# Graph-network kernel: rows of a block spread over partitions, and a rearranged first stage and turn

## The reference

```
x = relu(layernorm(x));  z = layernorm(x) * ln1_g + ln1_b
q, k, v = z @ Wq + bq, z @ Wk + bk, z @ Wv + bv          # 8 heads of 64
scores[e, h] = q[dst[e], h] . k[src[e], h] / 8 + edge_attr[e, h]
alpha = softmax of scores over the edges that share dst
out = segment_sum(alpha * v[src], dst) @ Wo + bo
```

## Time and profile before

| | us |
|---|---|
| median of 3 runs | 410.22 |
| profiled execution | 413.15 |
| its span, first to last instruction | 411.7 |
| PE busy in it | 379.6 (92%) |
| DVE busy | 317.4 (77%) |
| ACT busy | 166.7 (40%) |
| mean granted TensorE clock | 0.987 |

### The profile page before, as it was taken

The page is one execution under the profiler, slowest core; times in us unless marked ns, Lnnn a source line. Parts: engine busy times, 40 slices in busy tenths (PEclk is TensorE's granted clock), DMA queues, the critical chain, the costliest instruction groups (busy, mean ns, idle before and its releaser), DMA issues.

```text
span 411.7 us, 5093 instructions
## 1 busy us (share of the span) xinstructions
PE 379.6 (92%) x1785; PEld 286.7 (70%) x1785; DVE 317.4 (77%) x668; ACT 166.7 (40%) x274; POOL 2.2 (1%) x13
## 2 busy tenths in 40 slices
PE   2779998889899999999999999999799999999994
PEld 1555564456567788889767878887668878787873
DVE  5797998789893968899795988399875678488346
ACT  1624444534522623334655934243362631135410
POOL 2000000000000000000000000000000000000000
PEclk9999999999998999999999999999989999999989
DMA  7503786777882600006900060500230023000002
GB/s 240 228 1 59 103 104 102 111 99 97 116 107 57 228 0 2 1 2 211 369 35 1 0 205 0 204 2 0 64 142 0 2 75 130 0 2 0 2 0 102
DMA packets 16296, 32.92 MB, mean 80 GB/s; under 512 B 1360, under 2 KB 1488, under 8 KB 16272
## 3 DMA queue, kind: packets, MB, share of 16 engines
q1 hardware_dynamic: 15744, 32.25, 32.2%
q10 hardware_dynamic: 528, 0.36, 0.4%
HBM read 21.07 MB, written 1.05 MB: 54 GB/s over the span
## 4 chain that ended last, share of the span: by engine, by line
PE 70%; DVE 14%; DMA 5%; ACT 5%; issue 3%; SPq 0%; DVEq 0%; ACTq 0%
PE acc L1324 9%; PE bank L1306 8%; PE bank L1406 6%; PE bank L1208 6%; PE bank L1209 6%; DMA big<-z_sb 5%; PE bank L1189 4%; PE acc L1189 4%; PE acc L1208 4%; PE acc L1209 4%; PE bank L1391 3%; PE acc L1377 3%; DVE big_rounded L595 2%; PE acc L1166 2%; PE bank L1166 2%
## 5 line engine op out<-in xcount | busy, mean ns | idle before, releaser
L1324 PE MATMUL acc<-wide_rounded,c_rounded 128*126 128x512 f32 x200 | 60.3, 444 | 6.0 <-ACT acc L431 4.8
L1324 PEld LDWEIGHTS acc<-wide_rounded,c_rounded 128*126 128x126 f32 x200 | 37.8, 192 | 26.3 <-issue 19.1
L730 DVE TENSOR_SCALAR wide_rounded<-iota_f,picked 128x512 fp32r<-128x512 f32 x100 | 43.5, 481 | 9.9 <-PE acc L1324 8.7
L426 ACT COPY z_sb<-acc 126x512 f32<-126x512 f32 x37 | 21.7, 586 | 56.0 <-DMA big<-z_sb 26.8
L450 ACT ACTIVATE wide<-wide,low_col 128x512 f32<-128x512 f32 x32 | 21.4, 717 | 32.7 <-DVE low_col L844 32.7
L1406 PEld LDWEIGHTS bank<-v_sb,big 128*128 128x128 f32 x256 | 29.7, 192 | 4.7 <-issue 4.0
L568 DVE TENSOR_TENSOR wslot_rounded<-wslot,wide_rounded 128x512 fp32r<-128x512 f32 x24 | 16.2, 688 | 21.2 <-ACT wslot L359 21.2
L1406 PE MATMUL bank<-v_sb,big 128*128 128x65 f32 x256 | 31.6, 277 | 0.0
L736 DVE TENSOR_TENSOR c_rounded<-row_bc,wslot_rounded 128x1008 fp32r<-128x1008 bf16 x25 | 30.0, 1200 | 0.0
L1306 PE MATMUL bank<-t_sb,wslot 128*128 128x512 f32 x64 | 29.7, 596 | 0.0
L595 DVE TENSOR_TENSOR big_rounded<-big,big_rounded 128x1024 fp32r<-128x1024 f32 x24 | 29.1, 1222 | 0.5
(11 more groups left out here) (296 smaller groups left out, 770.1 us busy)
## 6 DMA issues: line engine op xcount, KB each, us to landing
big<-z_sb SPq DMA_DIRECT2D x33, 252.0 KB
big<-in_w SPq DMA_DIRECT2D x4, 2048.0 KB, 7.8
x_sb<-in_x SPq DMA_DIRECT2D x8, 256.0 KB, 5.2
big<-in_w_3t SPq DMA_DIRECT2D x2, 1024.0 KB, 6.6
row_bc<-in_rows SPq DMA_DIRECT2D x7, 256.0 KB, 6.3
wslot<-in_wq SPq DMA_DIRECT2D x1, 1024.0 KB, 9.1
wslot<-in_wk SPq DMA_DIRECT2D x1, 1024.0 KB, 11.0
wslot<-in_wv SPq DMA_DIRECT2D x1, 1024.0 KB, 13.0
```

Of the source, the lines that this page charges most:

```text
L426: nc.scalar.copy(stage[0:BROWS, b % STAGES, :], a).then_inc(S["staged"], 1)
L730: nc.vector.tensor_scalar(hot_ring[:, u, k, :], iota_f[:, :], picked[:, 0, s0 + k:s0 + k + 1], None, ALU.is_equal)
L1324: last = nc.tensor.matmul(to, st_ring[:, u, 2 * k + a, :, :].rearrange("p w k -> p (w k)"), hot_ring[:, u, k, :], start=False, stop=False, ...
```

## The change

Five things at once.

1. **Spread rows.** The 512 nodes lie in another order in every [node, ...] tile: x is handed over permuted and the result permuted back outside the kernel. In a tile of 128 partitions, block j of 9 has its 14 nodes on partitions j, j + 9, j + 18, ...; the last 2 partitions of the four tiles hold the 8 nodes of the 37th block. So 36 blocks are one DMA each to partitions 9 apart, and the block that goes first is four DMAs of 2 nodes. `iota_f` holds the node number of each position (five GpSimd instructions in place of one); a short table `steps` takes its place where plain numbers are needed.
2. **First stage shared.** ScalarE finds mean and variance of x for tiles 0 and 1 (sum by `accum_out`, square, scale), takes the high parts of the slot weights out of PSUM (`w_hi`), and does the second norm of tiles 2 and 3. The order of transposes is 0, 2, 1, 3 into banks 3, 0, 4, 5; PE zeroes banks 1 and 2 before them, ScalarE clears 3 and 0 as it takes t out.
3. **Bias by pairs of heads.** Bias on 128 partitions (edge tile and parity of the head) times 4 pairs; its exponentials are 4 of 128 partitions instead of 8 of 64, the weights 4 matmuls of 128 rows and 200 columns instead of 8 of 64 rows and 100 columns.
4. **Maximum first.** The turn and spread of the bias maximum come ahead of the slot tables on PE and DVE.
5. **Turn interleaved.** The transposes of the counts are split by column tile and put between the first scores, `e_turn(0)` and the third score unit; the wait for the last weights goes behind `scores(0)`, one `qkv_out` moves behind `lowest(0)`. Eight matmuls of zero use (`keep_warm(3, 8)`) stand before the z transposes, four of 384 columns in the loop's table.

```diff
         def block_parts(n):
             b = NBK - 1 - n
-            first, last = b * BW, min((b + 1) * BW, N)
-            cut = min((first // P + 1) * P, last)
-            parts = [((first // P, first % P, cut - first), 0)]
...
+            if b == NBK - 1:
+                return [((t, slice(TAKEN, P)), t * LEFT, LEFT) for t in range(NT)]
+            first = b % BLOCKS
+            return [((b // BLOCKS, slice(first, first + (BW - 1) * BLOCKS + 1, BLOCKS)), 0, BW)]
...
+            for t in range(NT):
+                nc.gpsimd.iota(node_of[:, t, 0:TAKEN].rearrange("p (i j) -> p i j", j=BLOCKS),
+                               [[1, BW], [BW, BLOCKS]], base=t * TAKEN, channel_multiplier=0,
...
-            act.sem_inc(S["evacuated"], ACC)
+            act.sem_inc(S["evacuated"], 2)
...
+            for t in range(2):
+                act.wait_ge(S[f"x_in{t}"], 16)
+                nc.scalar.activation(h_sb[:, t, :], x_sb[:, t, :], ACT.Identity, accum_out=x_sums[:, t:t + 1]
...
+            for t in range(2):
+                nc.scalar.activation(h_sb[:, t, :], x_sb[:, t, :], ACT.Square, bias=x_means[:, t:t + 1],
+                                     accum_out=x_squares[:, t:t + 1]).then_inc(S["x_sums"], 1)
...
-            for h in range(H):
-                nc.scalar.activation(att_b[:, h, :], att_b[:, h, :], ACT.Exp, bias=bmax_all[0:ET, h:h + 1]
+            for h in range(HP):
+                nc.scalar.activation(att_b[:, h, :], att_b[:, h, :], ACT.Exp, bias=bmax_all[:, h:h + 1]
...
+            act.wait_ge(S["weights_mm"], 1)
+            for q in range(2):
+                from_pe = bank[6 + q][:, 0:4 * SLOTS].rearrange("p (h s) -> p s h", h=4)
+                nc.scalar.copy(wp[:, 0:SLOTS, 0, 4 * q:4 * q + 4], from_pe).then_inc(S["w_hi"], 1)
             ln_stds(1)
+            act.wait_ge(S["ln_coef"], 2 * NT)
+            for t in (2, 3):
+                nc.scalar.activation(z_sb[:, t, :], h_sb[:, t, :], ACT.Identity, bias=shift[:, t:t + 1],
...
-            to_t(0, 2, t_sb, "ln1_g", "ln1_b")
+            z_turned(0)
+            z_turned(1)
+            act.wait_ge(S["t_ready"], 2)
+            clear(Z_BANKS[0])
+            z_turned(2)
+            z_turned(3)
+            clear(Z_BANKS[1])
...
-            zeros((0, 1))
+            zeros((1, 2)).then_inc(S["pair_mm"], 1)
             pe.wait_ge(S["rows_ready"], 1)
             held = choices(0, 2 * GROUP)
+            keep_warm(3, 8)
...
-            turn_by_row(z_sb, 2, "z_ready", 0, "turned")
-            pe.wait_ge(S["t_ready"], 2)
-            zeros((2, 3)).then_inc(S["pair_mm"], 1)
+            for i, t in enumerate((0, 2, 1, 3)):
+                pe.wait_ge(*((S["z_ready"], t + 1) if t < 2 else (S["z_scalar"], t - 1)))
...
-            pe.wait_ge(S["weights_read"], 2)
...
             scores(0)
+            pe.wait_ge(S["b_ready"], 1)
+            pe.wait_ge(S["weights_read"], 2)
+            counts_turn(0)
             scores(1)
-            pe.wait_ge(S["b_ready"], 1)
-            pe.wait_ge(S["qkv_ready"], 3 * NT)
-            turn(counts, 4, "c2_turned")
+            counts_turn(1)
             for n in range(UNITS + 1):
                 if n < UNITS:
                     e_turn(n)
+                if n == 0:
+                    pe.wait_ge(S["qkv_ready"], 3 * NT)
+                    counts_turn(2)
+                    counts_turn(3)
```

More of the change, by code:

```diff
@@ L21 @@
 H = 8
+HP = H // 2
 DH = D // H
@@ L30 @@
 BROWS = BW * KW
+BLOCKS = P // BW
+TAKEN = BLOCKS * BW
+LEFT = P - TAKEN
+assert NT * TAKEN + NT * LEFT == N and LEFT * NT <= BW and NBK == NT * BLOCKS + 1
 SLOTS = 100
@@ L129, in gnn_kernel @@
         rcnt_sb = sb("rcnt_sb", [P, N])
+        steps = rcnt_sb[:, 0:1 + SLOTS]
         def both(view, full, rounded):
@@ L276, in _ @@
                 sp.wait_ge(S["staged"], b + 1)
-                for (t, row, n), first in block_parts(b):
-                    sp.dma_start(by_head[row:row + n, t, :, :],
+                for (t, nodes), first, n in block_parts(b):
+                    sp.dma_start(by_head[nodes, t, :, :],
                                  stage[first * KW:(first + n) * KW, b % STAGES, :]
@@ L683, in slot_picks @@
                 dve.wait_ge(S["slots_mm"], r + 1)
-                nc.vector.tensor_tensor(pick[:, c], bank[4][0:ET, column(PICK)], slot1[:, c], ALU.is_equal
-                                        ).then_inc(S["picks_ready"], 1)
+                for a in range(2):
+                    half = slice(a * ET, (a + 1) * ET)
+                    last = nc.vector.tensor_tensor(pick2[half, a, c], bank[4][half, column(PICK)], slot1[half, c],
+                                                   ALU.is_equal)
+                last.then_inc(S["picks_ready"], 1)
                 nc.vector.tensor_single_scalar(rows_u[:, c], bank[4][0:1, column(NEEDS)], float(NBK + 1),
@@ L1258, in bias_turned @@
                 pe.wait_ge(S["bias_top"], 1)
-                nc.tensor.transpose(bank[6][0:H, 0:ET], bmax[0:ET, :], ident[0:ET, 0:ET]).then_inc(S["bias_turned"], 1)
+                nc.tensor.transpose(bank[6][0:HP, 0:P], bmax[:, 0:HP], ident[:, :]).then_inc(S["bias_turned"], 1)
             def bias_spread():
                 pe.wait_ge(S["bias_column"], 1)
-                nc.tensor.matmul(bank[6][0:ET, ET:ET + H], top_c[:, 0:1].broadcast_to([H, ET]), ident[0:H, 0:H],
-                                 start=True, stop=True).then_inc(S["bias_spread"], 1)
+                for a in range(2):
+                    last = nc.tensor.matmul(bank[6][a * ET:(a + 1) * ET, P:P + HP],
+                                            top_c[:, a:a + 1].broadcast_to([HP, ET]), ident[0:HP, 0:HP],
+                                            start=True, stop=True)
+                last.then_inc(S["bias_spread"], 1)
             def pair_table(r, c):
@@ L1338, in _ @@
             pair_table(0, slice(0, SLOTS))
-            zeros((0, 1))
+            zeros((1, 2)).then_inc(S["pair_mm"], 1)
             pe.wait_ge(S["rows_ready"], 1)
             held = choices(0, 2 * GROUP)
+            keep_warm(3, 8)
             pe.wait_ge(S["round_steps"], 2)
-            turn_by_row(z_sb, 2, "z_ready", 0, "turned")
-            pe.wait_ge(S["t_ready"], 2)
-            zeros((2, 3)).then_inc(S["pair_mm"], 1)
+            for i, t in enumerate((0, 2, 1, 3)):
+                pe.wait_ge(*((S["z_ready"], t + 1) if t < 2 else (S["z_scalar"], t - 1)))
+                for c in range(NT):
+                    last = nc.tensor.transpose(tile(bank[Z_BANKS[c]], t), tile(z_sb[:, t, :], c), ident[:, :])
+                    if i == NT - 1:
+                        last.then_inc(S["turned"], 1)
             for g in range(NG - 1):
@@ L1411, in _, with counts_turn @@
             pe.wait_ge(S["staged"], NBK)
+            def counts_turn(c):
+                for t in range(NT):
+                    last = nc.tensor.transpose(tile(bank[4 + c], t), tile(counts[:, t, :], c), ident[:, :])
+                last.then_inc(S["c2_turned"], 1)
             scores(0)
+            pe.wait_ge(S["b_ready"], 1)
+            pe.wait_ge(S["weights_read"], 2)
+            counts_turn(0)
             scores(1)
-            pe.wait_ge(S["b_ready"], 1)
-            pe.wait_ge(S["qkv_ready"], 3 * NT)
-            turn(counts, 4, "c2_turned")
+            counts_turn(1)
             for n in range(UNITS + 1):
@@ L1443, in degree_rows @@
                                      ).then_inc(S["deg_mm"], 1)
[L1445 removed]
+            turn_by_row(z_sb, 0, "z_ready", 2, "turned", between=degree_rows)
             product_in_parts(FF1_BANKS, weight("w1_0", NT), halves(t_at, t_lo), reads("ff_in"), "ff1_mm",
```

133 lines of the change are left out of this document (81 added, 52 removed).

## The result

The changed kernel takes **397.29 us** (median of 4 runs, 396.99 to 399.19), the kernel before in the same comparison 410.41 (4 runs, 409.74 to 412.86): ratio 0.968 [0.963, 0.973], 13.1 us less. Forecast were 396.8, in a range of 393 to 403. The profiled execution took 397.2 us, its span is 395.7 (before 411.7), its mean granted clock 0.992 (before 0.987).

A forecast was written before the change was run, and what follows sets the result against it. Mid-pairs, block DMAs hold ScalarE and through it PE (8.2 us of waits); before that the start is late. First stage 5.5 + pairs 7.5 + passage 0.4 = 13.4 us off the 410.22 median gives 396.8 us, range 393.0 to 403.0.

The forecast's parts named there:

- Bound: Middle of the pairs: ScalarE waits for block DMAs, PE for the cleared bank behind those copies; 8.2 us are PE waits.
- First stage: Start up to the first projection: begins at 26.1 instead of 31.67, 5.5 us gained; other end 3.6 us.
- The feared price of accumulation: ScalarE's statistics in the first stage: each accumulation might cost another 0.3 us, ending them at 11.3 instead of 10.1.
- Rival B: First projections slow again (start gain 3.6) and DVE delays the pairs' end to 115.5: 401.5 us, chance 0.15.
- DVE's slack of 0.9 us: Pairs: DVE's last left side at 109.2, needed by PE at 110.1, with DVE's third one-hots starting at 28.8.
- Pairs: First projection to last group: ends at 112.7, 7.5 of 8.2 us of waits come back; bounds 112.0 and 115.5.
- the 0.7 us for the ring: Pairs: wait added for a ring of two groups, moving the end from 112.0 to 112.7.
- the room above: Pairs: a block put at 0.8 us when spread, due every 2.3 us on average and 1.8 early.
- Passage: Pairs' end to first transposed exponentials: 8.3 us instead of 9.55, eight transposes (0.96) only move; gain 0.4, ends -0.5 and +1.5.
- C: Block DMAs: the spread does nothing, DMA engines hold 104 GB/s, only the earlier start gains: 405.9 us, chance 0.07.
- D: Block DMAs: the spread is slower, rows 9 apart colliding with partitions being read, 3.0 us a block: 425 us, chance 0.04.
- E: More gained: the passage gains its 1.5 and later waits shrink: 393 us or less, chance 0.08.

The follow-up runs named there:

- experiment 2: Kernel before with the spread rows alone, first stage, bias and passage as before: 403.76 us, ratio 0.9822.
- experiment 1: Changed kernel with each block's 14 rows on neighbouring partitions again, blocks still whole: 406.02 us, ratio 0.9894.
- experiment 3: Changed kernel with rows of 32 of the 36 whole blocks 2 partitions apart instead of 9: 403.81 us, ratio 0.9769.
- experiment 7: Changed kernel with scores, transposes of the counts and last outputs of v in the order of before: 396.58 us, ratio 0.9634.
- experiments 9 to 11: Changed kernel, counts' third column tile turned before the first transposed exponentials: with six extra matmuls 399.29 us, without 395.8, without on another chip 398.33.
- experiment 5: Changed kernel without the eight matmuls of no use before the z transposes: 398.61 us, ratio 0.9691.
- experiment 8: Changed kernel without the four matmuls of 384 columns in the loop's table: 400.97 us, ratio 0.9729.
- experiment 9: Changed kernel with the counts' third column tile turned before the first transposed exponentials, plus six matmuls of no use: 399.29 us, ratio 0.9683.

## Why the prediction was right

**Bound.** Right: the queue's DMAs held ScalarE, its clears held PE. With the rows spread the wait is gone (experiment 2), without the spread it stays (experiment 1).

**First stage.** `bias_low` 9.32 (forecast 9.7), first h 13.95 (14.2), z 19.68 (20.5), transposes done at 22.0 (22.4) at 2.4 GHz, first projection 25.59 (26.1). The feared price of accumulation was 0.19 us a pass. The forecast had ScalarE's statistics (10.1) end behind `bias_low` (9.7) and so set the pace; in the trace they end first, at 8.52, and ScalarE waits for DVE. The term, 5.5 us, came out as 6.1; but the row that it starts from, 31.67, held 2.1 us of late full speed, which experiment 2 gains without less work in this stage. If they are that execution's, as argued there, the term is 4.0 and 5.5 was too much. I took 3.41 us for the first group as the kernel's, where it was probably that execution's.

**Rival B** took the rule of the Trainium skill (TensorE: Matmul & The Clock Gate, Part 4: PE-mode transpose), that transposes don't count as busy, for a fall of the clock before the projections. The trace does not show one here: eight matmuls, a gap of 1.67 us, 1.7 us of transposes, the first group with a gap of 0.69 inside and one of 0.47 behind it, and the first projections run at full speed (14 records in 6.28 us, where half speed would be 0.86 each). Its other half, DVE's slack of 0.9 us, did not decide either, since DVE's third one-hots began at 27.88, not 28.8.

**Pairs.** 8.2 of 8.2 us came back (forecast 7.5); the 0.7 us for the ring was caution. A block costs 0.91 us, 0.8 was forecast; the room above (2.3 on average, 1.8 early) was large enough that 1.14 did nearly as well (experiment 3, 1.0 us of waits).

**Passage.** The one term that came out with the wrong sign. Its own numbers give 9.55 - 8.3 - 0.96 = 0.3, not 0.4. Measured up to the first transposed exponentials it is 7.72 us (forecast 8.3), but the eight transposes that moved behind were put at 0.96 us, full speed and nothing else. In the trace they run at half clock, and 4.92 us pass from the first to the second transposed exponentials, against 2.20 before. To the first `weighted` the passage is 0.9 us longer than before, outside the stated -0.5 to +1.5, and experiment 7 undoes the interleaving at no cost.

**Sum.** 13.4 forecast; 16.0 between the profiled executions, 13.1 between medians. The 16.0 are 6.1 (start) + 8.2 (waits) - 0.9 (passage) + 2.6 (clock behind it). Some 4.7 us of them, the 2.1 at the start and the 2.6 behind, are probably how the clock ran in these two executions, and 11.3 is left for the stages. Against these the forecast of 13.4 had 1.5 too much at the start and 1.3 in the passage, and 0.7 too little in the pairs. It hit by 0.5 us because the medians lie 1.8 us further apart than the stages account for, which the prediction had no reason to expect. That is luck. The clock may be in these 1.8 us too. Of the 10 runs of the changed kernel 5 have a mean clock of 0.991 or more, but only one of the 35 runs of the kernel before beside the experiments. What of the change would do that isn't shown. By the stages alone it would have been 399.1 us, still inside the range.

**Do the parts add up?** At the end of the pairs they do. The spread alone is 10.6 us earlier there than before, the rest alone 5.8, and together 14.2 (125.83 to 111.58); both single figures hold the 2.1 us of before, and without counting it twice the sum is 14.2 as well. In medians, 7.0 and 4.8 against 13.1, the difference of 1.3 is inside the scatter.

**Rivals C and D** fell with experiments 1 and 2; E's 393 was never seen (lowest of all runs 394.9).

## What to carry to other kernels

Which partitions the rows of a DMA go to can set its price: here a block of 2 KB rows took the engines 2.06 us on neighbouring partitions and 0.91 on partitions 9 apart. Read busy share and GB/s together; a high share at a low rate (0.73 at 104 GB/s) was the sign that spreading the partitions would pay. Before a first-stage term is taken from one trace, see in the times of the matmuls when PE reached full speed: that alone moved 2.1 us here. And measure a reordered passage up to where the moved work is done, not to the first instruction that comes earlier: 1.8 us gained became 0.9 lost.

## What the runs showed of the hardware

**The clock differs between executions by as much as small edits are worth.** Ten runs of the same changed kernel: 396.4 to 397.2 us at a mean clock of 0.991 to 0.996, 397.4 and 397.7 at 0.987 and 0.988, 399.2 and 399.6 at 0.983, 401.0 at 0.979. What a stretch at half clock costs depends on its place. The one at 119 us costs 1.9 us (experiments 9 to 11). One between 282 and 302 us costs 1.0 to 1.4. From the instruction at 366.09 in the changed kernel to the end the 7 profiles with a stretch some 13 us behind it, the one of before among them, take 31.1 to 31.3 us, the 7 without 29.6. The changed kernel's own stretch from 392 us on costs nothing, since PE is idle there.

**More PE work can be faster**: eight matmuls of no use gain 1.4 us at the start (experiment 5) and 1.2 in the median, and without four in the loop's table the median is 3.5 us higher (experiment 8, cause open). Six in the passage gain nothing (experiment 9).

**A DMA of one block alone takes 3.0 to 4.6 us** from the end of the copy to its landing, whatever the spacing: 3.04 (experiment 8, 112.08 to 115.12) and 4.63 (experiment 5, 113.68 to 118.31) with rows spread, 3.27 with rows eight apart, 4.51 with rows together (experiment 1). In all four the queue is empty before. In experiment 8 the engines move nothing for the first 1.4 us and then are busy for about 1. So behind the pairs the counts wait for latency, not for the rate.
